# Other slots for the side visits of a conv-attention and mixture-of-experts kernel, and two other ways to image 1's affinity exponentials

## What is computed

```python
sf   = xg.mean(axis=(3, 5))                      # 7x7 cells of 8x8 pixels
aff  = softmax(einsum('bnpc,bnck->bnpk', pix, sf9) * scale)   # pixel against its 9 neighbour cells
sft  = fold3(einsum('bnpc,bnpk->bnck', pix, aff)) / (aff_sum + 1e-12)
q, k, v = split(qkv_w @ sft)                     # 8 heads over 49 cells
out  = proj_w @ (v . softmax(k q)) + proj_b
x    = x + einsum('bnck,bnpk->bncp', unfold(out), aff)
```

```python
scores = ln(t) @ gate_w + gate_b;  masked = top-2 of softmax(scores), normalised
h = gelu(ln(t) @ w1[e] + b1[e]);  y = h @ w2[e] + b2[e]      # 96 -> 384 -> 96
t = t + sum_e masked[e] * y[e]
```

## Time and profile before

| | us |
|---|---|
| median of 3 runs | 578.9 (577.29 to 582.36) |
| the profiled execution, its own time | 574.71 |
| its span, first to last instruction | 572.8 |
| PE busy | 519.6 (91%) |
| DVE busy | 413.9 (72%) |
| ACT busy | 367.2 (64%) |
| POOL busy | 107.1 (19%) |
| mean granted TensorE clock | 0.951 of 2.4 GHz |

### The profile page before, as it was taken

How to read it: one execution, slowest core, us unless ns; L and a number is a source line. 1 busy time by engine, 2 the same in 40 slices (tenths; PEclk the granted TensorE clock), 3 DMA queues, 4 the chain that set the end, 5 groups by cost and what they waited for, 6 DMA issues and landing times.

```text
span 572.8 us, 14453 instructions
## 1 busy us (share of the span) xinstructions
PE 519.6 (91%) x6014; PEld 385.6 (67%) x6014; DVE 413.9 (72%) x1079; ACT 367.2 (64%) x365; POOL 107.1 (19%) x198
## 2 busy tenths in 40 slices
PE   8899997889898989898988989898988599998995
PEld 5886865766766767676666667675656387675655
DVE  7474957786876678787767687867787557878665
ACT  1053269658766567667766567757877557887873
POOL 2310012333101500415100600310101500111010
PEclk9668589999999999999999999999999789999999
DMA  8760020000000003000000000000000000000000
GB/s 251 230 175 2 2 66 20 15 17 1 16 15 2 15 16 87 15 10 7 15 1 15 16 7 11 17 1 15 15 17 2 15 15 3 16 15 16 15 15 17
DMA packets 15718, 17.51 MB, mean 31 GB/s; under 512 B 13781, under 2 KB 13917, under 8 KB 15262
## 3 DMA queue, kind: packets, MB, share of 16 engines
q1 hardware_dynamic: 14626, 14.86, 9.2%
q10 hardware_dynamic: 1028, 1.74, 1.1%
HBM read 11.78 MB, written 4.82 MB: 29 GB/s over the span
## 4 chain that ended last, share of the span: by engine, by line
PE 60%; ACT 14%; issue 8%; DVE 7%; POOL 7%; DMA 3%; SPq 0%; POOLq 0%; ACTq 0%; DVEq 0%
PE ps L1274 24%; PE ps L1303 10%; ACT h L653 7%; PE ps L1308 5%; PE ps L1139 4%; ACT hh L661 3%; PE ps L1126 3%; PE ps L1295 3%; DMA xt<-xtok 3%; PE ps L1106 2%; PE ps L1290 2%; POOL affr L231 2%; DVE xt L983 2%; ACT xhl L615 2%; POOL x L450 1%
## 5 line engine op out<-in xcount | busy, mean ns | idle before, releaser
L967 DVE TENSOR_TENSOR hl<-h,hh 128x1536 f16<-128x1536 f32 x94 | 169.6, 1805 | 31.5 <-issue 25.3
L1274 PE MATMUL ps<-xhl,w_hi 97*128 97x512 f16 (+1 forms) x672 | 177.9, 356 | 14.6 <-ACT xhl L615 14.6
L653 ACT ACTIVATE h<-ps 128x1536 f32<-128x1536 f32 (+1 forms) x100 | 142.4, 1424 | 64.8 <-PE ps L1274 64.4
L983 DVE SCALAR_TENSOR_TENSOR xt<-ps,gl,xt 128x96 f32<-128x96 f32 (+1 forms) x400 | 99.9, 309 | 67.5 <-PE ps L1308 58.6
L661 ACT CAST hh<-h 128x1536 f16<-128x1536 f32 x94 | 137.7, 1465 | 3.0
L1274 PE MATMUL ps<-xhl,w_lo 97*128 97x512 f16 (+1 forms) x336 | 114.9, 355 | 0.0
L1303 PE MATMUL ps<-w_lo,hh 128*128 128x96 f16 x1128 | 108.1, 207 | 0.0
L1303 PE MATMUL ps<-w_hi,hh 128*128 128x96 f16 x1128 | 108.1, 207 | 0.0
L450 POOL TENSOR_TENSOR x<-xs,x 128x384 f16<-128x384 f32 (+1 forms) x28 | 37.5, 1338 | 361.5 <-ACT x L608 361.5
L1303 PEld LDWEIGHTS ps<-w_lo,hh 128*128 128x128 f16 x1128 | 97.7, 98 | 6.3 <-issue 0.2
L1303 PEld LDWEIGHTS ps<-w_hi,hh 128*128 128x128 f16 x1128 | 99.0, 98 | 3.3
(11 more groups left out here) (160 smaller groups left out, 517.0 us busy)
## 6 DMA issues: line engine op xcount, KB each, us to landing
xch<-x SPq DMA_DIRECT2D x4, 1176.0 KB, 7.4
out<-xt SPq DMA_DIRECT2D x24, 192.0 KB, 2.1
xt<-xtok SPq DMA_DIRECT2D x4, 663.0 KB, 12.6
xt<-xtok SPq DMA_DIRECT2D x4, 612.0 KB, 10.9
h<-w ACTq DMA_DIRECT2D x2, 576.0 KB
wqkv_sb<-wqkv ACTq DMA_DIRECT2D x1, 228.0 KB
tab<-table ACTq DMA_DIRECT2D x1, 117.0 KB, 4.2
out<-xt SPq DMA_DIRECT2D x4, 24.0 KB, 1.8
```

What stands on the lines that cost most here:

```text
L653: act.activation(h32[:, i % 3, :, 0:width(i)], z, ACT.Gelu, scale=1.0 / WS).then_inc(S["h_ready"], 1)
L967: dve.tensor_tensor(hl[:, i % 2, :, 0:n], h32[:, i % 3, :, 0:n], hh[:, i % 3, :, 0:n], ALU.subtract).then_inc(S["hl_ready"], 1)
L983: ins = dve.scalar_tensor_tensor(out=xt[0:n, b, t, 0:C], in0=ps[0:n, Y, j * C:(j + 1) * C], scalar=gl[0:n, b % 2, t, e:e + 1], in1=xt[0:n, ...
L1274: ins = pe.matmul(ps[:, CH * (i % 2) + c, k * m:(k + 1) * m], ww[:, w0:w0 + 128], xhl[:, b % 2, half, r * UT:r * UT + m], start=(n == 0), ...
```

## The change

What changes:
- `TABLE` becomes EARLY plus a late part, and SHORT for images with no image b+2. SFT starts half a slot earlier, AFT 0 and 1 go from (8,0) and (8,1) to (10,1) and (11,0), PRT to PRO one slot earlier, PIX 0 to (11,1), TRN 4 from (14,0) to (12,0) and TRN 5 from (18,0) to (17,0), or (16,1) in SHORT. With SHORT the last PIX stands at (16,0) and not at (17,1).
- `NORMAL`: unit 5 in slot 10 (11 before), unit 6 in slot 12 (18 before).
- The wide multiply (L231) of images 1 to 3 goes from POOL to DVE, in slot 2; affinity_weights goes from DVE to POOL, in slot 3, as one instruction over all 25 tiles. affinities_high goes to slot 5, affinities_low to 6, attention_tanh to 6, attention_weights to 7.
- Statistics of image b+2 (25 bn_stats) are spread over slots 3, 4, 5, 6, 8; pixel_statistics follow their PIX; pixel_deviation is in slot 18, or 17 with SHORT; gate_ranks goes from slot 22 to 23.
- Image 1's exponentials: the first half before the slots, ahead of the load of Gelu's table; the second half in slot 0 as tanh, on ACT, and 1 - tanh, then on DVE in slot 2 a reciprocal and a multiply.
- Before the slots, TRN 0 goes ahead of the first part of LOG 1, and keep_busy(8) behind it is gone.

The diff, without lines that only declare or pass a name:

```diff
-NORMAL = {0: 2, 4: 3, 9: 4, 11: 5, 18: 6}
+NORMAL = {0: 2, 4: 3, 9: 4, 10: 5, 12: 6}
...
-        def scale_affinities(engine, k0, k1, between=None):
+        def scale_affinities(engine, k0, k1):
...
                                                [p1 - p0, last - k0, j1 - j0, K9]), ALU.mult)
-                if between and p0 == 0:
-                    between(ins)
...
                 (0, "PIX", 6): [((1, "SF", 3), 1, 0, 1), ((1, "CEN", 0), 0, 0, 1), ((1, "LOG", 0), Y, 0, 1),
-                                ((1, "LOG", 1), SIDE, 0, 2), ((0, "TRN", 0), 3, 0, 1)]}
+                                ((0, "TRN", 0), 3, 0, 1), ((1, "LOG", 1), SIDE, 0, 2)]}
...
-        TABLE = {(1, 1): (0, "TRN", 1), (3, 0): (0, "TRN", 2),
-                 (4, 0): (1, "SFT", 0, 0, 4), (4, 1): (1, "SFT", 0, 1, 4), (5, 0): (1, "SFT", 0, 2, 4),
-                 (5, 1): (1, "SFT", 0, 3, 4), (6, 0): (1, "SUPT", 0), (6, 1): (1, "QKV", 0), (7, 0): (1, "SCO", 0),
-                 (7, 1): (0, "TRN", 3), (8, 0): (1, "AFT", 0), (8, 1): (1, "AFT", 1), (9, 0): (1, "PRT", 0),
-                 (9, 1): (1, "HEA", 0), (10, 0): (1, "HET", 0), (10, 1): (1, "PRO", 0), (11, 0): (1, "PRO", 1),
-                 (11, 1): (1, "AFT", 2), (12, 0): (1, "PIX", 0), (12, 1): (2, "SF", 0), (13, 0): (1, "PIX", 1),
-                 (13, 1): (2, "SF", 1), (14, 0): (0, "TRN", 4), (14, 1): (1, "PIX", 2), (15, 0): (1, "PIX", 3),
-                 (15, 1): (2, "SF", 2), (16, 0): (1, "AFT", 3), (16, 1): (1, "PIX", 4), (17, 0): (1, "PIX", 5),
-                 (17, 1): (1, "PIX", 6), (18, 0): (0, "TRN", 5), (18, 1): (2, "SF", 3), (19, 0): (2, "CEN", 0),
-                 (19, 1): (2, "LOG", 0), (20, 0): (2, "LOG", 1), (20, 1): (0, "TRN", 6), (21, 0): (2, "LOG", 2),
-                 (22, 0): (2, "LOG", 3), (22, 1): (1, "TRN", 0)}
+        EARLY = {(1, 1): (0, "TRN", 1), (3, 0): (0, "TRN", 2),
+                 (3, 1): (1, "SFT", 0, 0, 4), (4, 0): (1, "SFT", 0, 1, 4), (4, 1): (1, "SFT", 0, 2, 4),
+                 (5, 0): (1, "SFT", 0, 3, 4), (5, 1): (1, "SUPT", 0), (6, 0): (1, "QKV", 0), (6, 1): (1, "SCO", 0),
+                 (7, 0): (0, "TRN", 3), (8, 0): (1, "PRT", 0), (8, 1): (1, "HEA", 0), (9, 0): (1, "HET", 0),
+                 (9, 1): (1, "PRO", 0), (10, 0): (1, "PRO", 1), (10, 1): (1, "AFT", 0), (11, 0): (1, "AFT", 1),
+                 (11, 1): (1, "PIX", 0), (12, 0): (0, "TRN", 4), (12, 1): (1, "PIX", 1), (20, 1): (0, "TRN", 6),
+                 (22, 1): (1, "TRN", 0)}
+        TABLE = {**EARLY, (13, 0): (2, "SF", 0), (13, 1): (1, "PIX", 2), (14, 0): (1, "AFT", 2), (14, 1): (1, "PIX", 3),
+                 (15, 0): (2, "SF", 1), (15, 1): (1, "PIX", 4), (16, 0): (1, "AFT", 3), (16, 1): (1, "PIX", 5),
+                 (17, 0): (0, "TRN", 5), (17, 1): (1, "PIX", 6), (18, 0): (2, "SF", 2), (18, 1): (2, "SF", 3),
+                 (19, 0): (2, "CEN", 0), (19, 1): (2, "LOG", 0), (20, 0): (2, "LOG", 1), (21, 0): (2, "LOG", 2),
+                 (21, 1): (2, "LOG", 3)}
+        SHORT = {**EARLY, (13, 0): (1, "AFT", 2), (13, 1): (1, "PIX", 2), (14, 0): (1, "PIX", 3), (14, 1): (1, "AFT", 3),
+                 (15, 0): (1, "PIX", 4), (15, 1): (1, "PIX", 5), (16, 0): (1, "PIX", 6), (16, 1): (0, "TRN", 5)}
+        def pixels_over(b):
+            return 17 if b + 2 < B else 16
...
-            entry = TABLE.get((slot, half))
+            entry = (TABLE if b + 2 < B else SHORT).get((slot, half))
...
-            def affinities_scaled(b):
-                pool.wait_ge(S["exp_ready"], 2 * b + 2)
+            def affinity_weights(b):
                 pool.wait_ge(S["scale_ready"], 2 * b + 2)
-                scale_affinities(pool, 0, PAIRS, ps1.link).then_inc(S["affr_ready"], 2)
+                pool.wait_ge(S["aff_hi"], 2 * b)
+                pool.wait_ge(S["aff_lo"], b)
+                pool.tensor_tensor(affn[:], aff[:, 0:T, :], affs[:, 1, 0:T].unsqueeze(2).to_broadcast([PT, T, K9]),
+                                   ALU.mult).then_inc(S["aff_ready"], 2)
...
                     if b + 1 < B:
-                        if slot == 2:
-                            affinities_scaled(b + 1)
-                        if slot == 5:
+                        if slot == 3:
+                            affinity_weights(b + 1)
+                        if slot == 6:
                             affinities_low(b + 1)
-                        if slot == 18:
+                        if slot == pixels_over(b) + 1:
...
                 act.activation(aff[:, t0:t1, :], aff[:, t0:t1, :], ACT.Exp).then_inc(S["exp_ready"], 1)
+            def affinity_tanh():
+                t0, t1 = half_tiles(1)
+                act.wait_ge(S["shifted"], 4)
+                act.activation(aff[:, t0:t1, :], aff[:, t0:t1, :], ACT.Tanh, scale=0.5).then_inc(S["aff_tanh"], 1)
+                act.wait_ge(S["aff_tanh"], 1)
+                act.activation(affd[:], aff[:, t0:t1, :], ACT.Copy, bias=1.0, scale=-1.0).then_inc(S["aff_tanh"], 1)
...
             gate_exponentials(0)
+            tokens_turned(0, 0)
+            affinity_exponentials(1, 0)
             act.activation(scrap[:, 5:6], scrap[:, 0:1], ACT.Gelu)
-            tokens_turned(0, 0)
...
                     if i == 0:
-                        affinity_exponentials(1, 0)
-                        affinity_exponentials(1, 1)
-                    if slot == 3:
+                        affinity_tanh()
+                    if slot == 5:
                         affinities_high(b + 1)
-                    if slot == 7:
+                    if slot == 6:
...
+            def affinity_quotient():
+                t0, t1 = half_tiles(1)
+                dve.wait_ge(S["aff_tanh"], 2)
+                n1.link(dve.reciprocal(affd[:], affd[:]))
+                dve.scalar_tensor_tensor(out=aff[:, t0:t1, :], in0=aff[:, t0:t1, :], scalar=1.0, in1=affd[:], op0=ALU.add,
+                                         op1=ALU.mult).then_inc(S["exp_ready"], 1)
...
-            def affinity_weights(b, k):
+            def affinities_scaled(b):
+                dve.wait_ge(S["scale_ready"], 2 * b + 2)
+                dve.wait_ge(S["side_done"], number[(b - 1, "SFT", 0)] + 1)
+                scale_affinities(dve, 0, PAIRS).then_inc(S["affr_ready"], 2)
+            def first_weights(k):
                 t0, t1 = half_tiles(k)
-                dve.wait_ge(S["scale_ready"], 2 * b + k + 1)
-                if b > 0:
-                    dve.wait_ge(S["aff_hi"], 2 * b)
-                    dve.wait_ge(S["aff_lo"], b)
+                dve.wait_ge(S["scale_ready"], k + 1)
...
             affinity_shift(1)
-            affinity_weights(0, 0)
+            first_weights(0)
...
             affinities_scaled_first(1)
-            affinity_weights(0, 1)
+            first_weights(1)
...
             gate_logits(0)
+            logits(1, 0)
+            affinity_shift(0)
             normalise(0, 1)
-            logits(1, 0)
...
             gate_weights(0)
-            affinity_shift(0)
...
                     side_read(first)
-                if b + 1 < B and slot == 22:
-                    gate_ranks(b + 1)
...
                 if b + 1 < B:
+                    if i == 2:
+                        affinity_quotient()
...
                         affinity_sums(b + 1, slot - 1)
-                    if slot == 3:
-                        affinity_weights(b + 1, 0)
-                        affinity_weights(b + 1, 1)
-                    if slot == 8:
+                    if slot == 2:
+                        affinities_scaled(b + 1)
+                    if slot == 7:
                         attention_weights(b + 1)
-                    if 12 <= slot <= 17:
-                        pixel_statistics(b + 1, slot - 12)
-                    if slot == 17:
-                        pixel_statistics(b + 1, 6)
+                    for v in (first, second):
+                        if v and v[1] == "PIX":
+                            pixel_statistics(b + 1, v[2])
...
                         normalise(b + 1, 1)
+                    if slot == 23:
+                        gate_ranks(b + 1)
...
                 if b + 2 < B:
-                    if slot in (4, 5, 6, 7):
-                        statistics(b + 2, {4: 0, 5: 5, 6: 12, 7: 18}[slot], {4: 5, 5: 12, 6: 18, 7: T}[slot])
+                    if slot in (3, 4, 5, 6, 8):
+                        statistics(b + 2, *{3: (0, 8), 4: (8, 12), 5: (12, 17), 6: (17, 20), 8: (20, T)}[slot])
...
                 side(v, part, parts)
-                if v == (0, "TRN", 0):
-                    keep_busy(8)
```

More of the change, by code:

```diff
@@ L188, in build @@
         affn = sb("affn", [PT, T, K9])
+        affd = sb("affd", [PT, T - HALF_T[1], K9])
         affs = sb("affs", [PT, 3, PAIRS * TR])
@@ L248, in build @@
             ones_in zeros_set pool_set ident16_set gatew_done gatew_set w_hi weights_set
-            cell_ready stats_done pixels_done shifted exp_ready scale_ready aff_ready affr_ready
```

(1 more changed line is left out.)

## The result

The median went from 579.24 us (4 runs of the kernel before, 577.29 to 582.36) to 549.12 us (4 runs, 547.32 to 550.83): ratio 0.9475 [0.9416 to 0.9534]. The forecast was 551 in a range of 541 to 565. The profiled execution took 547.52 us, where the sum had 548.2.

What follows compares the result with a forecast made beforehand. PE was taken as the bound, with 10.25 us of gaps per image; -13.8 - 13.2 + 0.6 + 0.9 - 1.0 = -26.5 us from 574.7 gave 548.2, plus 2.8 made 551 us, range 541 to 565.

Steps and rivals of the forecast that it cites:

- TRN 4 and 5: First layer's waits for ACT's xhl copy: eight of nine, two per image, go with TRN placed earlier, 13.8 us gone.
- The end of an image: Slots 20 to 23: pixel_deviation's chain starts earlier, DVE's wait goes, image 2's gap falls from 6.12 to 0.8; 13.2 us gained.
- The middle: Slots 7 to 12: splitting the AFT pair saves 1.47, ACT's order adds new waits; +0.2 per image, +0.6 us in all.
- The wide multiply: Slot 2, moved to DVE: meeting POOL's affinity_weights it takes 3.0 us, SFT waits 2.1; +0.9 us over images 1 and 2.
- The rival without any meeting: DVE and POOL don't meet at the multiply and two thirds of ACT's new waits are hidden: 543 us, chance 0.16.
- The start: Before the slots and slots 0 to 2: second_layer(3) and the first SFT part done at 102.0, not 103.0; gain 1.0 us.
- the clock stays low: Rival: without keep_busy the clock stays at its lower level from first_layer(0) on; slower, fifteen slots give 600; chance 0.04.
- The first Gelu: Slot start: expected at 76.3 us and not 78.0, if the clock rises at 75.4 as now.
- The offset: Runs' median against the profiled execution: 4.2 us above it before, 2.8 added to the sum of 548.2.
- DVE as a bound in slots 2 to 8: Rival: DVE's 35.2 us against PE's 34.3 in images 0 and 1, stalls 3 longer per image: 560 us, chance 0.20.
- The waits that did move on: Rival: TRN copies and DVE reads land where PE next wants the bank, half of 27 comes back: 565 us, chance 0.08.
- My signs of being wrong: Three: L1290 waits in slots 4 to 9, PE gaps above 7 us per image, clock at 0.50 after 79 us.

Runs made afterwards that it cites:

- e1: The kernel before with only TRN 4 moved to (13,1) and TRN 5 to (15,1), SF 1 and SF 2 taking their places: 562.87 us, ratio 0.9718.
- e2: The kernel before with only NORMAL's unit 6 in slot 12 and not 18: 567.26 us, ratio 0.9767.
- e9: e4 with NORMAL's unit 4 in slot 8 and not 9, unit 5 in slot 11 and not 10: 542.61 us, ratio 0.9363.
- e4: The changed kernel with POOL's affinity_weights also waiting until DVE's wide multiply is done: 544.75 us, ratio 0.9441 to the kernel before.
- e5: The changed kernel with 20 unread matmuls ahead of the first SFT part of image 1: 548.45 us, ratio 0.9487 to the kernel before.
- e8: The changed kernel with keep_busy(8) and the old order of LOG 1 and TRN 0 back: 550.68 us, ratio 0.9483 to the kernel before.
- e3: The kernel before with the edits of e1 and e2 together: 553.47 us, ratio 0.9549.
- e7: The changed kernel with the wide multiply back on POOL and affinity_weights back on DVE: 558.11 us, ratio 0.9637 to the kernel before.
- r_after: The changed kernel run once more, unaltered, beside e4, e5 and another experiment on their chip: 548.38 us, ratio 0.9509 to the kernel before.

## Why the prediction was right

- **TRN 4 and 5, -13.8.** Right in place and size: L1299 has no idle time at all. e1 shows the mechanism alone, though there four new waits of 0.40 to 0.64 come in. The ninth wait (0.8) went too, which I had left in.
- **The end of an image, -13.2.** Right: 2.91 to 0.17 in images 0 and 1, 6.12 to 1.03 with the clock at full speed in image 2 (2.74 twice, 5.09 and 2.3 are 12.9). The reason was right as well: e2 shows that the chain behind tokens_low was what was late, and that DVE's own load in slots 20 to 23 is next. My 0.8 for that load was an estimate without a sum: the terms beside it add up to 5.65 against 4.0. Measured were 0.23 and 0.80.
- **The middle, +0.6.** 1.47, 0.66 and HEA's 0.3 were replaced by 0.34, 1.07 and 1.12, so +0.1 per image where I had +0.2. Each new wait stood where I had put it: PRT 0.34 (0.5 forecast), AFT 0 1.07 (1.16), PIX 0 1.12 (1.0). e9 confirms why: without tokens_high ahead of them two shrink by 0.4.
- **The wide multiply, +0.9.** The meeting with POOL was right and its price too high. The multiply took 2.38 and not 3.0, PE's wait 1.43 and not 2.1, about what it was before. I had let the meeting hold more than one instruction; it held one, 243 elements, by 1.13 us (e4). The rival without any meeting fell with e4.
- **The start, -1.0.** The one term that was wrong: the state that should have come 1.0 earlier came 0.4 later. The step that failed is not DVE's schedule: SFT began at 98.11, where mine has the multiply done at 99.0. What failed is that I gave the pair of SFT part and second layer its full-clock time, though by my own schedule PE waits for DVE ahead of it until 99.0. SFT took 2.30 and not 1.25; e5 shows 2.4 us given back when that gap is filled. I had this price in the bounds, and in the rival "the clock stays low", but tied it to keep_busy, which e8 shows to be beside the point.
- **The first Gelu** came at 76.13, where I had 76.3, but that doesn't show my reason for it. e1 and e3 keep keep_busy(8) and the old order, and theirs came at 76.33 and 76.15. What differs is when the clock rises: at 73.8 and 73.6 in these two, at 76.6 in the kernel before (I took 75.4, where my row merely ends), at 76.2 in the changed one. That this number fits is luck.
- **Images 0 and 1 as a whole** gained 6.5 each where the terms gave 5.6. By gaps 0.5 of it is the multiply (1.49 to 1.43, where I had 0.45 more) and 0.1 the middle; 0.3 is PE's own busy time (120.85 and 120.55), which no term had.
- **The offset.** I added 2.8 to the execution's time for the median; it was 1.6. The sum (548.2) is 0.7 over the profiled execution, so the 1.4 that the start lacked was more than made up by images 0 and 1 (0.9 each) and the end (0.2). The mechanisms of the large terms are shown; that the sum comes so near is in part luck, by errors that cancel.
- **The rivals.** DVE as a bound in slots 2 to 8 needed waits at L1315 in slots 4 to 9, and it has none there; that line waits 4.8 in the whole span, and an image has 4.13 of gaps. (The rival of a clock that stays low has a slip: fifteen slots at 1.2 GHz give 551 + 54 = 605, not 600.) The waits that did move on are the 2.5 per image of "The middle", which the sum had.
- **My signs of being wrong.** One of the three came: the clock was to be 0.50 nowhere after 79 us, and it is 0.50 from 96.7 to 103.6. It is the step of "The start" again, and its price is 2.4 us. The other two stayed away: no waits at L1315 in slots 4 to 9, 4.13 us of gaps per image and not 7.

## What to carry to other kernels

Where a pipeline waits at many places, put at least half a slot between a small piece of side work and the layer that reads it (that was enough for TRN 4 in e1), and look at what the queues ahead of a slow chain hold: five table entries gave 26 us here (e3, 21 to 31), where the whole change gave 30 (ratio 0.9475 of 579). When two engines are released by one signal and read the same memory, order them; and where a wait as long as the 3.6 us here is left on PE, count the lower clock behind it (2.4 us) as well as the gap.

## What the runs showed of the hardware

- A DVE tensor_tensor over 243 elements takes 405 ns alone and 1535 ns beside a POOL tensor_tensor that starts 0.3 us ahead of it and takes 1.58 us. DVE's first instruction of four, which had begun before POOL's, is not held (496 ns in the changed kernel and in e4). By the Trainium skill, page SBUF: State Buffer, section Who interferes with whom, such instructions hold each other off for a whole instruction. The trace agrees: when the second DVE instruction begins at 223.20, POOL's has 1.27 us to go, and DVE's takes 1.13 longer than alone. The changed kernel shows it once more, in two executions of one instruction of 100 elements. At 68.14 POOL's L459 runs beside it (from 68.03, 0.91 us), at 190.89 POOL is idle:

```profile
68.14 0.92 DVE L925 TENSOR_TENSOR gl<-gl,gs 128x100 f32<-128x100 f32 x1
190.89 0.26 DVE L925 TENSOR_TENSOR gl<-gl,gs 128x100 f32<-128x100 f32 x1
```

- In the changed kernel the granted clock fell from its level of 2.4 GHz to 1.2 at 96.7 us, inside a PE gap of 3.56 us that ends at 98.11, and was up again at 103.6. e2 has one fall near a gap of 1.86 us, where the same gap in the kernel before has none:

```profile
287.60:294.50 6.90, 5.14 (x25) 2.56 (x26) 3.08 (x7) 3.15 (x3) 0.00 (x0) 0.66 0.00 0
```

- In e4 it fell at 102.2, behind a gap of 2.42 us; in e1 at 326.3, in a gap of 1.25 us that the kernel before passes at full clock. No fall shows at the 2.85 of e9, and of e7's two gaps of 3.19 us one has a fall and one has none. So the length of the gap alone doesn't tell whether the clock falls.
- Ahead of the slots the clock is at its lower level in stretches that differ between executions of one kernel: in the execution of e4 to 81.6 us, in that of r_after to 76.3. With the old start it ends at 76.6 in the kernel before, at 78.1 in e2 and at 73.6 in e3. That is probably part of why the runs of the kernel before range from 573 to 583 us; it was not isolated.
